# Two softmaxes of a self attention: the multiplication by the reciprocal sums goes from DVE to ACT

## The reference, cut to what matters

```
Q, K, V = split(x_norm @ c_attn_w + c_attn_b)          # 256 wide each
scores  = Q K^T * SCALE
p       = softmax(scores)                              # first softmax
cam     = tanh((p V)[:, first 128] * cam_gate)         # a gated context
bias    = cam K_cam^T * (SCALE * layer_weight)
final   = softmax(scores + bias)                       # second softmax
out     = (final V) @ c_proj_w + c_proj_b
```

## Time and profile before

| | |
|---|---|
| median of 3 runs | 854.81 us |
| profiled execution | 849.15 us, its span 847.4 us |
| busy over the span | PE 83%, DVE 70%, ACT 48%, POOL 43% |
| mean granted clock of PE | 0.935 of full speed |
| self attention with two softmaxes | from about 164 to 218.7 us of the span |

### The profile page before, as it was taken

How to read it: one execution, slowest core, us unless ns; L and a number is a source line. 1 busy time by engine, 2 the same in 40 slices (tenths; PEclk the granted TensorE clock), 3 DMA queues, 4 the chain that set the end, 5 groups by cost and what they waited for, 6 DMA issues and landing times. The chain is left out here.

```text
span 847.4 us, 16539 instructions
## 1 busy us (share of the span) xinstructions
PE 700.3 (83%) x5485; PEld 468.2 (55%) x5488; DVE 595.7 (70%) x1139; ACT 406.9 (48%) x1283; POOL 367.5 (43%) x309
## 2 busy tenths in 40 slices
PE   4996898787357469998996899668999999999586
PEld 3664666576214345343433566436777777777444
DVE  3556788567677646565665778568788888888567
ACT  1556777343255121231213777336555555555574
POOL 3401454128144113333453545249566676666200
PEclk9999999999787559999999999989999999999979
DMA  8452000000200012302001300012221212220301
GB/s 248 142 178 102 2 0 0 1 2 1 87 1 0 1 31 76 87 1 87 1 1 44 107 0 0 18 40 57 58 50 48 55 55 57 57 57 20 150 1 50
DMA packets 33562, 41.80 MB, mean 49 GB/s; under 512 B 15072, under 2 KB 23264, under 8 KB 32608
## 3 DMA queue, kind: packets, MB, share of 16 engines
q1 hardware_dynamic: 33504, 41.06, 16.6%
HBM read 40.00 MB, written 1.05 MB: 48 GB/s over the span
## 5 line engine op out<-in xcount | busy, mean ns | idle before, releaser
L1716 POOL TENSOR_TENSOR ra_direct<-ra_direct,ra_crossed 128x512 f32<-128x512 f32 x64 | 81.1, 1268 | 68.1 <-DVE ra_crossed L1875 68.1
L689 POOL TENSOR_TENSOR c_probs<-c_probs,c_inverse 128x512 f32<-128x512 f32 x64 | 66.0, 1039 | 77.5 <-DVE c_inverse L705 77.4
L1321 POOL TENSOR_TENSOR r_turned<-r_times_a,r_times_b 128x1024 f32<-128x1024 f32 x24 | 56.4, 2349 | 95.3 <-DVE r_times_b L1505 95.3
L1875 DVE SCALAR_TENSOR_TENSOR ra_crossed<-bank,ra_bias,ra_sin 64x512 f32<-64x512 f32 x128 | 96.0, 750 | 1.9
L664 ACT ACTIVATE c_probs<-bank,c_neg_max 128x128 f32<-128x128 f32 x256 | 89.7, 384 | 5.3 <-DVE c_neg_max L723 5.3
L664 ACT ACTIVATION_READ_ACCUMULATOR c_probs<-bank,c_neg_max 128x1 f32 x256 | 57.7, 225 | 0.0
L1572 POOL TENSOR_TENSOR ra_w_lo<-ra_raw,ra_w_hi 128x768 f16<-128x768 f32 x32 | 52.5, 1644 | 9.9 <-ACT ra_w_hi L1565 9.9
L1832 ACT ACTIVATE ra_probs_t<-bank 64x256 f32<-64x256 f32 x64 | 24.2, 378 | 66.6 <-PE bank L1788 66.3
L1875 DVE SCALAR_TENSOR_TENSOR ra_direct<-bank,ra_bias,ra_cos 128x512 f32<-128x512 f32 x64 | 47.6, 743 | 8.3 <-PE bank L58 5.7
L58 PE MATMUL bank<-xt_hi,ra_w_hi 128*128 128x512 f16 x128 | 49.3, 385 | 2.9 <-PEq L547 2.9
L1838 ACT ACTIVATE ra_probs<-ra_masked,ra_neg_max 128x64 f32<-128x64 f32 x128 | 43.0, 336 | 17.9 <-DVE ra_neg_max L1895 17.9
(11 more groups left out here) (245 smaller groups left out, 2084.0 us busy)
## 6 DMA issues: line engine op xcount, KB each, us to landing
ra_raw<-l_attn_w_dram SPq DMA_DIRECT2D x32, 384.0 KB, 3.1
wq<-l_wq_dram SPq DMA_DIRECT2D x16, 256.0 KB, 2.9
wo<-l_wo_dram SPq DMA_DIRECT2D x16, 256.0 KB, 3.4
wkcq<-l_wkcq_dram SPq DMA_DIRECT2D x16, 192.0 KB, 3.1
ra_wo<-l_attn_wo_dram SPq DMA_DIRECT2D x1, 2048.0 KB, 10.1
wqr<-l_wqr_dram SPq DMA_DIRECT2D x16, 96.0 KB, 3.1
x_res<-x_dram SPq DMA_DIRECT2D x2, 512.0 KB, 4.9
wkv<-l_wkv_dram SPq DMA_DIRECT2D x16, 64.0 KB, 3.0
```

What stands on the lines that cost most here:

```text
L689: nc.gpsimd.tensor_tensor(out=probs[u][:, at, :], in0=probs[u][:, at, :], in1=inverse[u][:, at].unsqueeze(2).broadcast_to([P, HP, L]), op= ...
L1321: nc.gpsimd.tensor_tensor(out=turned[k % 3][:], in0=times_a[k % 2][:], in1=times_b[k % 2][:], op=ALU.add).then_inc(rotated, 1)
L1716: nc.gpsimd.tensor_tensor(out=direct[e][k][:], in0=direct[e][k][:], in1=crossed[k][:], op=ALU.add).then_inc(roped, 1)
L1875: ins = nc.vector.scalar_tensor_tensor(dst[out_lo:out_lo + rows].rearrange("p t (b s) -> p (t b) s", b=2), src[lo:lo + rows], bias[e][lo:l ...
```

## The change

The multiplication of `probs[w]` by `inverse[w]` moves from DVE (`tensor_scalar`) to ACT (an activation Copy with the reciprocals as a per-partition scale). On ACT it stands behind both exponentials of its step and ahead of `tanh`, and in step 0 ahead of the last `size_of`. DVE keeps the reciprocal alone, now called `invert`, and does it ahead of `keep_qk` rather than behind it. `invert` has a new wait for the previous `normed[w]`.

```
@@ ACT
+            def softmax_norm(w, t):
+                act.wait_ge(inverted[w], t + 1)
+                nc.scalar.activation(probs[w][:], probs[w][:], ACT.Copy, scale=inverse[w][:]).then_inc(normed[w], 1)
...
                 if has(i - 2):
                     softmax_exp(1, i - 2, i)
+                if has(i):
+                    softmax_norm(0, i)
+                if has(i - 2):
+                    softmax_norm(1, i - 2)
                 if i == 0:
                     prep.size_of(act, 2)
@@ DVE
-            def softmax_norm(w, t):
+            def invert(w, t):
                 dve.wait_ge(exped[w], t + 1)
+                wait(dve, normed[w], t)
                 nc.vector.reciprocal(inverse[w][:], total[w][:]).then_inc(inverted[w], 1)
-                dve.wait_ge(inverted[w], t + 1)
-                nc.vector.tensor_scalar(probs[w][:], probs[w][:], inverse[w][:], None,
-                                        ALU.mult).then_inc(normed[w], 1)
...
                 if i == 0:
                     ln.statistics(dve, 1)
+                if has(i):
+                    invert(0, i)
+                if has(i - 2):
+                    invert(1, i - 2)
                 if has(i + 1):
                     keep_qk(i + 1)
-                if has(i):
-                    softmax_norm(0, i)
-                if has(i - 2):
-                    softmax_norm(1, i - 2)
```

## The result

The changed kernel takes 847.78 us in the median of 20 runs (841.41 to 855.47), the kernel before 854.06 in 20 runs on the same chips (849.46 to 861.63). The ratio is 0.9933, with a 95% interval of 0.9913 to 0.9953: 4.0 to 7.4 us saved, 5.7 in the middle. That is inside the 1% which the prediction called no change, but in this comparison it is apart from zero. Forecast were 3.4 us and 851.4.

What follows compares the result with a forecast made beforehand. PE bounds an undisturbed step; DVE multiplications held by POOL passes make it wait. 0.88 + 1.31 + 2.03 - 0.20 - 0.62 - 0.05 = 3.35 saved, so 854.81 - 3.4 = 851.4 us, range 846.5 to 857.5.

Steps and rivals of the forecast that it cites:

- The cause: L964 on DVE, started inside a POOL pass, is held until the pass ends: 1.81 us instead of 0.29.
- Steps 5 to 9: Stage steps after the change: gains of 0.88, 1.31 and 2.03 us in 5 to 7, losses of 0.20 and 0.62 after.
- The cover by PE's projections in steps 3 to 6: PE's projections stand between there, so the added 0.6 us of ACT cost nothing.
- the price of 0.40 us on ACT: Each of 16 added 128x128 multiplications on ACT: 0.39 us like L910, with 0.40 as upper bound.
- the spacing of 0.30: On ACT the next instruction can start some 0.1 us before a multiplication ends, so 0.30 us apart.
- Steps 0 and 1: Start of the stage: `size_of` queued behind the multiplication on ACT, mostly hidden; a loss of 0.05 us.
- L1000 unlocked in step 5: The remaining DVE multiplication would start at 193.13, 0.07 us ahead of POOL's pass, and not be held.
- L1000 takes over the waits: Rival: POOL holds L1000 on DVE instead, losing 2.5 of the 3.4 us: 853.9; chance 0.22 in part or whole.
- The slower rival: Longer ACT chain delays `output` in all steps; nine lose 5.8 us: 855.7, or 858.2 with L1000's waits; chance 0.08.
- The sum: Whole stage: 0.88 + 1.31 + 2.03 - 0.20 - 0.62 - 0.05 = 3.35 us saved.
- the gross relief of steps 5 and 6: Their excess over an undisturbed step of 4.78 us, removed by the change: 0.88 and 1.31 us.

Runs made afterwards that it cites:

- second profile: Both kernels run again with no edit: stage 54.82 us before, 48.01 after; in that second comparison the change saves 3.0 us (0 to 6.0).
- order only: Kernel before with reciprocals and multiplications, still on DVE, moved ahead of `keep_qk`: 854.50 us in one execution, stage 53.59.
- summing form: Kernel before with the `probs` multiplication on DVE at its old place, in a form that also sums its output: 843.33 us, ratio 0.9909, stage 47.61.
- summing form, cam too: Kernel before with the DVE multiplications of both `probs` and `cam` in the form that also sums its output: 843.96 us, ratio 0.9862, stage 46.22.
- POOL shifted: One memset more on POOL ahead of its passes: kernel before 845.23 us, stage 51.43; kernel after 841.48 us, stage 47.46; one execution each.

## Why the prediction was right

By its steps. **The cause** was right: the plain multiplication of DVE is held up by a POOL pass. Taking the passes away gives 4.78, 4.78 and 3.84 for steps 5 to 7, and changing only the form of the instruction frees it.

**Steps 5 to 9** were forecast at 4.78, 4.78, 4.57, 4.01 and 6.15 and came out at 4.84, 4.78, 4.48, 3.99 and 6.17. The cover by PE's projections in steps 3 to 6, its absence in 7 to 9, the price of 0.40 us on ACT and the spacing of 0.30 all hold: in step 5 `tanh` starts 0.63 us behind the first of the two multiplications (192.84 against 192.21). The lower figure of the Trainium skill (VectorE: DVE Perf Modes, the TRN2 errata), an estimate of 0.29, is too low for the duration, 0.401 in the median. The end of the stage came at 215.35 against 215.3.

**Steps 0 and 1** were forecast to lose 0.05 and gained 0.35: step 0 fell from 4.14 to 3.78. `size_of` moved to 170.74 and cost nothing, as said, but I held the next M to its old time, though the first `turn` no longer waits for DVE's multiplication behind `keep_qk`. Before and after:

```profile
170.93 0.33 PE L841 MATMUL bank<-ident_sb,sa_probs 128*128 128x128 f32 x1 [1.58 <-DVE sa_probs L964]
```

```profile
170.88 0.33 PE L841 MATMUL bank<-ident_sb,sa_probs 128*128 128x128 f32 x1 [1.09 <-ACT sa_probs L915]
```

These 0.4 us are nearly all by which the stage beat its forecast (3.78 against 3.35).

**L1000 unlocked in step 5** was wrong: it was locked for 1.68 us, since POOL began at M0 + 25.02, 0.8 earlier than before. Its slack hid all but 0.06. In steps 6 to 8 it was to start inside a pass; only step 6 did so (0.80 us), 7 and 8 fell into gaps (0.28 and 0.29). By the starts of the passes in the first trace the releases there would also have come 0.2 to 0.3 us later than the +3.2, +2.65 and +2.1 of the prediction, still ahead of what `score` needs. The rival "L1000 takes over the waits" is true as a mechanism and nearly free; its largest price seen in the changed kernel is 0.5 us in step 7 of the second profile (4.99 against 4.48):

```profile
210.62 1.76 DVE L1006 TENSOR_SCALAR sa_cam<-sa_cam,sa_layer_weight 128x128 f32<-128x128 f32 x1 [0.72 <-ACT sa_cam L938]
```

```profile
212.52 0.68 PE L58 MATMUL bank<-sa_qk 128*128 128x128 f32 x4 [0.27 <-DVE sa_cam L1006]
```

The slower rival, the ACT chain reaching `output` in every step, is what happens when the reciprocals stay behind `keep_qk` (52.05): the moved `invert` is what keeps it off.

**The sum**, 3.4, lies below the first comparison (5.7, 4.0 to 7.4) and beside the second (3.0, 0 to 6.0). Against the stage of the profile that it was made from it was good: 3.35 against 3.78. Against the second profile of the kernel before it is mis-sized, and the term is the gross relief of steps 5 and 6, 0.88 + 1.31 = 2.19 as taken from the one profile. In the second profile of the same code it is 2.65 + 3.05 = 5.70, part of it the lower clock that followed the waits; with that value the sum gives 6.9, beside the 6.8 between the two second profiles. I had seen that the first L964 cleared POOL by 0.07 us and used it only to place L1000 after the change, not to ask what the kernel before pays when it misses.

How often it misses stays open, but the first profile looks like the rare case. The first L964 starts 2.14 us after M5, and the first pass there started 2.21 after M5. It started 1.87 after M5 in the second profile, and 1.49, 1.09 and 2.04 in the profiles "order only", "summing form" and "summing form, cam too", whose POOL code is the same; in "POOL shifted" it was 2.44, which without the added memset would be some 1.4, an estimate. What each of these phases costs the unchanged kernel wasn't measured. That the forecast fell as near as it did is therefore in part luck of the profile, and whether the rest of the 5.7 us is this alone was not shown.

## What to carry to other kernels

When an instruction has a median of 288 ns and a maximum of 1971, look at what another engine runs in the same microseconds, and by how much the lucky instances cleared it: a margin of 0.07 us is a coin, not a fact of the kernel. Moving the work to an engine without the conflict helped here only because it also landed in a slot where that engine has cover. The cheaper cure may be another form of the same instruction: used for `probs` alone it gave the same stage as the change (47.61), for `cam` too 46.22. And where the cover ends (here with the last projections), reorder: it gave 1.9 us of stage on top of the change.

## What was not expected of the hardware

Between two POOL passes lies about 0.1 us (195.25 to 195.33 in the earlier trace rows), and one waiting DVE instruction gets through there, with one queued directly behind it at times (195.25 in the earlier trace rows); a second one with a reciprocal in between doesn't, and waits for the next whole pass (1.88 us at 195.22 in the second profile of before). So two multiplications of 0.29 us took up to 3.9 (1.96 and 1.89, step 7 of the kernel before with the new order). And the clock makes a stall dearer: in the kernel before with the new order PE ran step 8 at a mean of 0.58 of full speed after waiting through steps 6 and 7, and the step took 4.78 us instead of 3.36.
